# Cross attention in a decoder kernel: all value products of a head pair in one step of four, and the context's probabilities transposed at full width

## The reference

```
x = layer_norm(ctx_1024);  l = layer_norm(latents)          # latents: the 512 tokens
q = l @ Wq;  k, v = split(concat([x, l]) @ Wkv)             # 544 keys
w = softmax((q * scale) @ (k * scale).T)                    # 4 batches, 16 heads, 512 x 544
out = (w @ v) @ Wo
```

## Time and profile before

| | us |
|---|---|
| median of 3 runs (lowest, highest) | 1845.26 (1844.14, 1848.06) |
| the profiled execution, its own time | 1845.25 |
| its span, first to last instruction | 1843.4 |
| TensorE busy | 1653.6 (90%) |
| VectorE busy | 1271.4 (69%) |
| ScalarE busy | 949.4 (52%) |
| GpSimd busy | 304.5 (17%) |
| granted TensorE clock, mean | 0.957 of full speed |

### The profile page before, as it was taken

How to read it: one execution, slowest core, us unless ns; L and a number is a source line. 1 busy time by engine, 2 the same in 40 slices (tenths; PEclk the granted TensorE clock), 3 DMA queues, 4 the chain that set the end, 5 groups by cost and what they waited for, 6 DMA issues and landing times.

```text
span 1843.4 us, 24921 instructions
## 1 busy us (share of the span) xinstructions
PE 1653.6 (90%) x8074; PEld 736.0 (40%) x8074; DVE 1271.4 (69%) x2994; ACT 949.4 (52%) x2053; POOL 304.5 (17%) x465
## 2 busy tenths in 40 slices
PE   7899999999999989999899988444798899999998
PEld 3355455545544432222244331222443355444443
DVE  7576666767667768888565578999666677762423
ACT  3565556556645516666633566333236366664333
POOL 1000000000001021121277200000000222114443
PEclk9999999999999989999999999777799799999999
DMA  4000000000000220240000000000100512100000
GB/s 193 1 1 1 1 1 1 1 1 1 1 1 21 55 59 23 73 116 2 1 0 1 0 1 1 1 1 1 69 1 1 147 55 73 32 2 1 1 0 23
DMA packets 19806, 44.36 MB, mean 24 GB/s; under 512 B 3872, under 2 KB 13024, under 8 KB 18912
## 3 DMA queue, kind: packets, MB, share of 16 engines
q1 hardware_dynamic: 19200, 42.39, 7.6%
q10 hardware_dynamic: 480, 0.39, 0.1%
HBM read 32.74 MB, written 9.44 MB: 23 GB/s over the span
## 4 chain that ended last, share of the span: by engine, by line
PE 75%; DVE 16%; ACT 5%; issue 3%; POOL 1%; DMA 0%; ACTq 0%; POOLq 0%; SPq 0%; DVEq 0%
PE ps L675 8%; PE ps L639 8%; PE ps L653 6%; PE ps L1226 6%; PE ps L1264 5%; PE ps L1112 5%; PE ps L1699 3%; PE ps L1700 3%; PE ps L596 3%; PE ps L1596 3%; PE ps L1612 3%; PE ps L1707 3%; DVE arena L2063 2%; PE ps L684 2%; DVE arena L2050 2%
## 5 line engine op out<-in xcount | busy, mean ns | idle before, releaser
L1390 DVE TENSOR_REDUCE stat<-ps 128x1 f32<-128x512 f32 (+3 forms) x512 | 279.1, 581 | 86.6 <-PE ps L1116 43.0
L1321 ACT ACTIVATE arena<-ps 128x512 f32<-128x512 f32 (+3 forms) x512 | 247.1, 515 | 154.3 <-PE ps L1264 83.3
L826 DVE TENSOR_REDUCE stat<-ps 128x1 f32<-128x544 f32 x256 | 173.4, 719 | 163.0 <-PE ps L639 163.0
L777 ACT ACTIVATE arena<-ps,stat 128x544 f32<-128x544 f32 x256 | 180.7, 711 | 201.9 <-DVE stat L826 201.9
L1264 PE MATMUL ps<-arena 75*128 75x512 bf16 (+1 forms) x480 | 163.1, 344 | 11.7 <-ACT arena L1321 9.5
L1112 PE MATMUL ps<-arena 72*128 72x128 bf16 (+1 forms) x480 | 163.0, 348 | 8.0 <-DVE stat L1390 7.8
L675 PE MATMUL ps<-arena 128*64 128x512 f32 (+1 forms) x640 | 159.2, 609 | 4.7 <-DVE arena L845 3.3
L639 PE MATMUL ps<-arena 64*128 64x272 f32 x1024 | 152.1, 415 | 5.1 <-ACT arena L777 4.3
L785 ACT COPY arena<-ps 128x512 f32<-128x512 f32 x256 | 137.3, 594 | 15.5 <-PE ps L653 15.5
L653 PEld LDWEIGHTS ps<-wA_sb,arena 128*128 128x128 f32 x1024 | 115.1, 142 | 70.1 <-issue 68.9
L653 PE MATMUL ps<-wA_sb,arena 128*128 128x128 f32 x1024 | 138.3, 278 | 0.0
(11 more groups left out here) (391 smaller groups left out, 2775.2 us busy)
## 6 DMA issues: line engine op xcount, KB each, us to landing
arena<-b_parts SPq DMA_DIRECT2D x180, 96.0 KB
b_parts<-arena SPq DMA_DIRECT2D x64, 128.0 KB, 1.9
reg<-wM_dram SPq DMA_DIRECT2D x1, 3072.0 KB, 10.0
reg<-wB_dram SPq DMA_DIRECT2D x1, 2048.0 KB, 12.4
reg<-wM_dram SPq DMA_DIRECT2D x1, 2048.0 KB, 16.7
reg<-wD_dram SPq DMA_DIRECT2D x1, 1817.0 KB, 10.7
wF_sb<-wF_dram SPq DMA_DIRECT2D x1, 1476.0 KB, 19.8
reg<-b_parts SPq DMA_DIRECT2D x12, 96.0 KB
```

The source lines that it names most:

```text
L777: e.activation(prob_of(P, r).rearrange("p (a k) -> p a k", a=2), score_banks(r), ACT.Exp, bias=x_neg[:, at_:at_ + 1], accum_out=x_sums[:, ...
L826: e.tensor_reduce(x_neg[:, n % 4:n % 4 + 1], score_banks(r), AX.XY, ALU.max, negate=True).then_inc(sem("max_done"), 1)
L1321: e.activation(p_t[:, m % 8, q0:T], ps[:, S1 + m % S2, q0:T], ACT.Exp).then_inc(exp_done, 1)
L1390: e.tensor_reduce(nm[:, G % 2, u // 4, u % 4:u % 4 + 1], ps[:, step % S1, 0:keys(u)], AX.X, ALU.max, negate=True).then_inc(max_done, 1)
```

## The change

- The transposition of the context's probabilities takes 128 columns from column 512 on in place of 64, and writes all 128 partitions of bank 6. The upper 64 are not used.
- All five parts of the value products are issued together at the end of step r = 3 (i = 4g + 7); the issues at r = 0 and r = 1 are gone.
- VectorE's read of them (`pv_read`) moves from r = 1 (i = 4g + 9) to r = 0 (i = 4g + 8). The order of the uses of bank 7 is as before.
- SyncE waits, before it writes the ones rows of the second buffer, also until GpSimd has split batches 0 and 1 (`split_q` and `split_k` at 8).

```diff
-                    e.transpose(ps[0:2 * S, 6, q * 128:q * 128 + 128], x_prob[:, P % 3, T:T + 2 * S],
+                    e.transpose(ps[:, 6, q * 128:q * 128 + 128], x_prob[:, P % 3, T:T + 128],
                                 ident).then_inc(sem("ctx_turned"), 1)
...
-                    if r == 1:
-                        if 0 <= (i - 9) // 4 < XP:
-                            pv((i - 9) // 4, (4,))
...
                     if r == 3 and 0 <= (i - 7) // 4 < XP:
-                        pv((i - 7) // 4, (0, 1))
-                    if r == 0 and 0 <= (i - 8) // 4 < XP:
-                        pv((i - 8) // 4, (2, 3))
+                        pv((i - 7) // 4, (0, 1, 2, 3))
+                        pv((i - 7) // 4, (4,))
...
-                    if r == 1 and 0 <= (i - 9) // 4 < XP:
-                        pv_read((i - 9) // 4)
+                    if r == 0 and 0 <= (i - 8) // 4 < XP:
+                        pv_read((i - 8) // 4)
...
                             if a and early is not None:
                                 e.wait_ge(sem("pv_done"), XP)
+                                e.wait_ge(split_q, 8)
+                                e.wait_ge(split_k, 8)
```

## The result

The changed kernel takes 1893.76 us (median of 5 runs, 1893.33 to 1898.91) against 1845.26 (5 runs, 1843.44 to 1848.06): a ratio of 1.0273, 95% interval 1.0257 to 1.0289. It is 48.5 us slower; the forecast was 45.0 us slower, at 1890.3. The profiled execution is the longest of the five, 1898.91 us.

A forecast was written before the change was run, and what follows sets the result against it. TensorE was taken to bound every step, just above a 3.53 us loop of scores, maxima and exponentials. Terms 80.0 - 17.7 - 19.5 - 3.0 + 7.4 + 1.8 - 4.0 = +45.0 us gave 1890.3 us, range 1876 to 1908.

The forecast's parts named there:

- second limit: Cross attention: the loop of scores, row maximum, exponential, next scores floors a step at 3.53 us.
- The value products in r = 3: Step number modulo 4 = 3: six pairs arrive, 2.58 us uncovered in each of 31 steps (7 to 127), +80.0 us.
- Steps r = 0 and r = 1: Emptied steps fall to 3.53 us: 30 by 0.59, -17.7 us; 26 by 0.75, -19.5 us.
- The three with an output projection: Three long steps r = 1 keep the whole 1.00 us gained from the context part: -3.0 us.
- The push into r = 2: ScalarE's late bank 7 reads delay the query projection: +0.39 us behind 10 roots, +0.29 behind 12 copies, +7.4 us.
- The knock-on to r = 3: Five chain statistics at r = 3 wait for VectorE behind the later projection, about 0.35 us each: +1.8 us.
- The tail: From step 128 on, without scores or loop: plain sum of pieces leaving and arriving, -4.0 us, between 0 and -6.6.
- The full width: Context's transposition with 128 instead of 64 weight columns streams the same 128 columns: cost 0.
- The read on VectorE: Bank 7 read (0.68 us) moved to r = 0 hides behind the maxima: 0; early release hidden by the floor anyway.
- SyncE's wait: Added wait for POOL's eight splits, which end at 671.20, before the ones rows go out at 673.86: 0.
- The faster one (TensorE's work alone): Rival, 6%: only TensorE's work counts, fewer block entries and exits gain, 1832.5 us; needs a floor under 2.91 us.
- The falling clock: Rival, 12%: idling lowers the granted clock, 1.7 us lost each time; 1907 us in a third of pairs, 1941 in all.

The follow-up runs named there:

- e8: Kernel before the change, plus an idle 128 x 256 copy on ScalarE ahead of the first head's exponential (longer loop): 1845.1 us, ratio 1.0003 to before.
- e9: Changed kernel plus the same idle 128 x 256 copy on ScalarE in the loop: 1911.4 us, ratio 1.0368 to before.
- e3: Kernel before the change, with each row's maximum taken over the first 272 of 544 scores only: 1828.1 us, ratio 0.9906 to before.
- e4: Changed kernel with only the four parts of 128 keys at r = 3, context part and VectorE's read left at r = 1: 1880.8 us, ratio 1.0190 to before.
- e7: Changed kernel with ScalarE's bank 7 reads (value copies, roots) for r = 1's uses taken ahead of that step's evacuations: 1891.0 us, ratio 1.0232 to before.
- e1: Kernel before the change, with only the full-width context transposition and SyncE's added waits: 1844.3 us, ratio 1.0001 to before.
- e5: Changed kernel with VectorE's read of the value products put back to r = 1, behind the maxima: 1915.1 us, ratio 1.0374 to before.

## Why the prediction was right, point by point

**The bound.** That a TensorE 99% busy stood only 0.6 us above a second limit was the reading on which all rested, and it held: r = 0 and r = 1 stopped at 3.53 us in nearly every pair, and e8 with e9 shows that the loop bounds one kernel and not the other. What the reading had wrong is "TensorE bounds every step". e3 shows waits for bank 7 in r = 1, 2 and 3 of the kernel before. They were too short to stand out in TensorE's idle times: the modelled ends of the matmuls cover them, and for r = 1 they show only in the row of the weight loads, as 0.2 us each.

**The value products in r = 3.** Forecast 2.58 us a step, measured 2.71 to 2.72. The parts 2 and 3 cost 1.72 (e4), as four times 0.43; the context part costs 1.00, not 0.86. In the run its first pair starts 0.56 us after the last pair of 128 keys, and its second 0.48 after that, where 0.43 is usual. The prediction's own row had the 1.00 (415.39 - 414.39), which it took for what leaves r = 1 and not for what arrives in r = 3. That is 30 x 0.14 = 4.2 us on the slow side.

**Steps r = 0 and r = 1.** -17.7 and -19.5 us, as measured. The three with an output projection lost 1.17 us each and not 1.00, because the 0.17 us wait for the read went too. In the others this could not be seen, the floor being above 3.28 and above the true 3.11.

**The push into r = 2.** Right in kind, e7; sized 0.39 and 0.29, measured 0.30 (4.64 to 4.65) and 0.20 (4.54). The query projection started at 1.64, not 1.73: ScalarE began the root 0.78 us after the scores, not 0.92, since its two evacuations overlap. With 10 and 12 cases that is 5.4 us, not 7.4. The knock-on to r = 3 (+1.8) did not occur: 7.90 is 5.19 + 2.71.

**The tail.** Forecast -4.0, and with step 127's own 2.58 a difference of -1.4 for the stretch. It was +1.0, so that the steps from 128 on gave 1.7 us and not 4.0. The two traces show where, if times are counted from the scores of step 127 (645.39 before, 688.64 after). Step 127 adds 2.72. The pieces gone from 128 and 129 gave 2.48 of their 2.87: the run of step 131 starts 0.24 us later than before. It adds 2.73. The piece gone from 132 gave nothing. A later product of TensorE waits there for GpSimd, whose splits start when VectorE has read the key product (L1100) that TensorE issues behind step 131's run. GpSimd's first split and that product, before and then after:

```profile
665.03 0.61 POOL L1337 CAST arena<-arena 128x512 bf16<-128x512 f32 x1 [4.45 <-DVEq L1370]
...
672.42 0.39 PE L1131 MATMUL ps<-wt_bf,arena 128*12 128x128 bf16 x4 [0.54 <-POOL arena L1457]
```

```profile
711.25 0.62 POOL L1333 CAST arena<-arena 128x512 bf16<-128x512 f32 x1 [7.18 <-DVEq L1366]
...
718.65 0.59 PE L1127 MATMUL ps<-wt_bf,arena 128*12 128x128 bf16 x4 [1.83 <-POOL arena L1453]
```

The split starts 2.97 us later (711.25 - 688.64 against 665.03 - 645.39), the product 2.98, and TensorE idles 1.83 us before it in place of 0.54. The prediction looked at VectorE's wait in step 132 and not at this one. The piece gone from 133 gave 0.87, and 1.08 came back in the output projection (L684), more of which ran at the full clock. That last term is chance: with the products unmoved the stretch took 42.10 us before and 42.65 in e1.

**The full width, the read on VectorE, SyncE's wait.** The first and the last cost nothing, as forecast (e1). The read costs nothing where it now is, and more than that: put back, it costs 17.5 us (e5, low-clock steps taken off). The prediction took bank 7's early release to be hidden by the floor; without it r = 1 would have stayed at 4.28 and not have reached the floor.

**The sum.** With the measured sizes: 30 x 2.72 - 30 x 0.59 - 26 x 0.75 - 3 x 1.17 + 5.4 = 46.3 us against 44.9 measured in the stage. The kernel before has 1.5 us there that the one after does not, in step 118, at a lower clock. The forecast has +49.0 without the tail, or 46.4 without step 127's own 2.58, and that this meets 46.3 is luck: the value products came out 4.2 us heavier and the three long steps gave 0.5 more, while the push was 2.0 lighter and the knock-on (1.8) nothing. The tail gave 2.3 us less than forecast. Stage and tail together carry 45.9 of the 48.5 us between the medians; what the other 2.6 are was not isolated, and the later stages differ by more than that from execution to execution.

Two smaller things in the text of the prediction: its lower bound of 1876 does not follow from its own terms (without the push and the knock-on, and with its best tail, they give 1878.5), and the last scores started at 688.64, not near 694, which had counted step 127's own run and a stage that began as early as before.

**The rivals.** The faster one (TensorE's work alone) failed on the floor, as was said: 3.53 and not under 2.91. The 0.20 us into the value products, which the prediction read as the price of a new shape, is there after the narrow transposition, whose weights are 128*64 as theirs are, and after the full-width one (e1) alike, so it does not show such a price. Clearer are the scores, which start 0.52 us after the last product where 0.43 is usual, and the context part inside the run. The rule of the Trainium skill, TensorEngine Tiling (Array Packing), Key Properties, that a change of tiling mode drains the engine, is not contradicted by these; no run isolates it. In a step that ends with a wait, a border less is worth nothing. The falling clock did not come either: the mean clock of the stage is 1.00 with, and 0.99 before the change. The row at 582 to 590 us on which that rival rested is step 114, with its 2.2 us of waiting; some 56 steps with 1.21 or 0.35 us of waiting brought no such fall.

## What to carry to other kernels

Before moving work between the steps of a loop, find in the trace a step in which nothing but the dependency cycle runs, and compare its length with the steps that you want to empty: only the part above it can be gained, while the step that receives the work pays in full. Work spread so that each step stays just above the cycle was cheaper here than the same work in one run, even though the run itself is shorter (2.72 us in place of 1.87 + 1.00). And ask for each read of a shared buffer what stands ahead of it in the reader's list: here some 14 us lay in reads and other work that stood behind row maxima, on an engine that was idle nearly a third of the stage.

## What the runs showed of the hardware

Later stages, whose instructions are the same, differ from execution to execution with the granted clock. The stretch from the experts' first matmul to the end took 930.56 us at a mean clock of 0.93 before, and 937.11 at 0.92 after. The longer loop on the kernel before (e8) gave the extreme in its profiled execution, which took 1858.6 us beside a median of 1845.1:

```profile
912.99:1856.70 943.71, 808.13 (x3692) 359.81 (x3688) 627.98 (x1809) 429.69 (x913) 232.10 (x275) 0.91 0.07 20
```

The narrow attention's stretch took 225.3 us at a clock of 1.00, 226.9, or 228.2 at 0.98, and the last of these in e3 too, which has none of the change's edits. So 6.6 + 2.9 of the 53.7 us between the two profiled spans are not the change's, and a difference of some 10 us between two single profiles of this kernel says nothing by itself. The stage's own length, cut at the same instructions, agreed to 0.1 us between before and e1 (585.6 and 585.7), which have the lower clock in the same steps.

At the lower clock a transposition starts 0.21 us after the one before it (586.03 to 586.89 in step 114 of the kernel before), and at the full clock 0.11 us.

A transposition of float32 costs TensorE the same 0.11 us with 64 or 128 weight columns: 119.30 to 119.41 in e3, and 442.12 to 442.23 in the changed kernel.
